# Moving the transfers of the negated maxima from SyncE's queue to ScalarE's in a fused cross-attention and feed-forward kernel

## The reference, cut to what matters

```python
def xattn(q, k, v):            # q = layernorm(x); k = v = ctx; each (16, 128, 256)
    # 8 heads of 16 rows each; positions are the 256 columns
    qh = q.reshape(16 * 8, 16, 256); kh = k.reshape(16 * 8, 16, 256); vh = v.reshape(16 * 8, 16, 256)
    qk = einsum('bdm,bdn->bmn', qh, kh) / sqrt(128 // 8)
    return einsum('bmn,bcn->bcm', softmax(qk, axis=-1), vh).reshape(16, 128, 256)

x = x + xattn(layernorm(x), ctx, ctx)
x = x + routed_expert(layernorm(x), ...)      # top 128 rows for each of 16 experts
x = x + masked_attention(layernorm(x), ctx, mask)
x = x + routed_ffn(layernorm(x), ...)         # top 64 of 128 rows in each batch
```

## Time and profile before

| | |
|---|---|
| median of 3 runs | 457.11 us (456.21 to 458.71) |
| profiled execution | 457.2 us |
| its span | 455.4 us |
| TensorE busy | 350.1 us, 77% |
| VectorE busy | 318.7 us, 70% |
| ScalarE busy | 170.2 us, 37% |
| SyncE's queue (q1) | 32.59 MB, 30.7% of 16 DMA engines |
| ScalarE's queue (q10) | 32 packets, 0.01 MB |
| transfers of the maxima | 30 on SyncE, 2 on ScalarE |
| transfers into the query stack, line 257 | 48 of 128 KB, 7.1 us from issue to landing (median) |

### The profile page before, as it was taken

How to read it: one execution, slowest core, us unless ns; L and a number is a source line. 1 busy time by engine, 2 the same in 40 slices (tenths; PEclk the granted TensorE clock), 3 DMA queues, 4 the chain that set the end, 5 groups by cost and what they waited for, 6 DMA issues and landing times.

```text
span 455.4 us, 7666 instructions
## 1 busy us (share of the span) xinstructions
PE 350.1 (77%) x1872; PEld 204.9 (45%) x1872; DVE 318.7 (70%) x989; ACT 170.2 (37%) x397; POOL 94.4 (21%) x222
## 2 busy tenths in 40 slices
PE   0054997998989999999999994100156999999996
PEld 0021442443534544445444442000134888888884
DVE  6755473887688778886788544788747788878641
ACT  3201553454536444554434441000011355565622
POOL 1101303304214133141110100000013333332300
PEclk9999998999999999999999996555555799999999
DMA  3887591480652815717100009000000000000001
GB/s 95 193 194 126 135 182 21 133 147 18 180 84 69 186 23 143 135 52 153 29 25 1 2 2 356 12 0 1 0 0 2 1 14 11 23 23 23 23 24 48
DMA packets 24363, 32.87 MB, mean 72 GB/s; under 512 B 4066, under 2 KB 22418, under 8 KB 22802
## 3 DMA queue, kind: packets, MB, share of 16 engines
q1 hardware_dynamic: 24306, 32.59, 30.7%
q10 hardware_dynamic: 32, 0.01, 0.0%
HBM read 24.02 MB, written 8.39 MB: 71 GB/s over the span
## 4 chain that ended last, share of the span: by engine, by line
PE 44%; DVE 17%; DMA 16%; issue 8%; SPq 6%; POOL 4%; ACT 3%; DVEq 0%; ACTq 0%; POOLq 0%
PE pv_bank L1041 15%; DMA q_stack<-neg_max 9%; PE t_bank L1247 5%; PE pv_bank L1165 5%; DMA q_parts_dram<-q_parts 4%; PE scoret_bank L1027 4%; PE score_bank L1014 4%; SPq L257 3%; PE t_bank L1069 2%; DMA q_stack<-q_parts_dram 2%; PE score_bank L1228 2%; PE score_bank L1195 1%; DVE junk L668 1%; SPq L238 1%; DVE equal L668 1%
## 5 line engine op out<-in xcount | busy, mean ns | idle before, releaser
L1041 PE MATMUL pv_bank<-probs,values_ones 128*32 128x256 f32 x512 | 135.5, 390 | 0.0
L517 DVE TENSOR_REDUCE row_max<-score_bank 128x2 f32<-128x512 f32 x112 | 75.9, 679 | 54.1 <-PE score_bank L1014 53.0
L858 ACT ACTIVATE probs<-scoret_bank 128x512 f32<-128x512 f32 x128 | 74.4, 593 | 73.9 <-PE scoret_bank L1027 72.9
L1041 PEld LDWEIGHTS pv_bank<-probs,values_ones 128*32 128x32 f32 x512 | 46.0, 110 | 54.4 <-issue 25.7
L1027 PE MATMUL scoret_bank<-q_stack,k_stack 98*128 98x256 bf16 (+1 forms) x256 | 50.3, 279 | 15.8 <-DMA q_stack<-neg_max 13.0
L1014 PE MATMUL score_bank<-k_stack,q_stack 96*128 (+1 forms) x240 | 48.7, 289 | 9.8 <-DMA q_stack<-q_parts_dram 9.8
L357 POOL TENSOR_SCALAR var_eps<-mv 128x1 f32<-128x1 f32 x48 | 9.2, 192 | 191.9 <-DVE mv L553 108.8
L1014 PEld LDWEIGHTS score_bank<-k_stack,q_stack 96*128 (+1 forms) x240 | 17.1, 100 | 48.5 <-issue 24.7
L1027 PEld LDWEIGHTS scoret_bank<-q_stack,k_stack 98*128 98x128 bf16 (+1 forms) x256 | 24.1, 99 | 27.8 <-issue 20.0
L1165 PE MATMUL pv_bank<-q_stack,k_stack 128*128 (+1 forms) x256 | 36.1, 285 | 0.4 <-ACT q_stack L990 0.4
L1165 PEld LDWEIGHTS pv_bank<-q_stack,k_stack 128*128 128x128 f32 x256 | 33.8, 202 | 1.3 <-issue 0.9
(11 more groups left out here) (182 smaller groups left out, 540.6 us busy)
## 6 DMA issues: line engine op xcount, KB each, us to landing
q_stack<-q_parts_dram SPq DMA_DIRECT2D x48, 128.0 KB, 7.1
k_parts_dram<-k_parts SPq DMA_DIRECT2D x24, 128.0 KB
q_parts_dram<-q_parts SPq DMA_DIRECT2D x24, 128.0 KB
k_stack<-k_parts_dram SPq DMA_DIRECT2D x8, 384.0 KB, 4.5
ctx_stage<-in_ctx_dram SPq DMA_DIRECT2D x8, 256.0 KB, 3.3
x_stage<-in_x_dram SPq DMA_DIRECT2D x8, 256.0 KB, 4.1
k_stack<-k_parts_dram SPq DMA_DIRECT2D x8, 256.0 KB, 5.2
xs<-in_x_dram SPq DMA_DIRECT2D x8, 256.0 KB, 2.7
```

The costliest lines, as they stand in the source:

```text
L517: dve.tensor_reduce(row_max[:, i, :, h], score_bank[h % 2][:, :].rearrange("p (m n) -> p m n", m=2), AX.X, ALU.max).then_inc(s["max_done"], 1)
L858: act.activation(probs[:, j % 4, :], scoret_bank[j % 2][:, :], ACT.Exp).then_inc(s["exp_done"], 1)
L1041: ins = pe.matmul(pv_bank[i][pair * Q:(pair + 1) * Q, odd * D:(odd + 1) * D], values_ones[:, i, k, pair, odd, :], probs[:, j % 4, k * D:(k ...
```

## The change

SyncE no longer issues any transfer of the maxima. ScalarE issues all of them, each pair behind a wait for `neg_done`: the odd batch's in step 2, between the exponential and `take_xnt`, and the next unit's even batch's in step 11, behind the exponential. The opening pair stays where it was, written with the new helper. The query stack's six pieces of 16 rows are as before; only the unused variable `n` goes.

```diff
@@ SyncE: load_stacks and the unit @@
-                n = NH * 2 * D
                 sp.dma_start(k_to[0:3 * C], k_rows).then_inc(s["stacks_loaded"], 16)
...
                 for block, part in enumerate((0, 0, 0, 1, 1, 2)):
                     sp.dma_start(q_to[block * C:(block + 1) * C], q_rows[part]).then_inc(s["stacks_loaded"], 16)
-
-            def load_neg_max(u, i):
-                wait_apart(sp, s["neg_done"], 2 * u + i + 1)
-                for part in range(2):
-                    sp.dma_start(q_stack[QROWS + part:QROWS + part + 1, u % SLOTS, :, i, :],
-                                 neg_max[:, i, part, :]).then_inc(neg_loaded[i], 16)
...
             def unit(u, more_stage, more_parts, more_x, reused):
-                load_neg_max(u, 1)
                 if more_x:
...
                     load_stacks(u + 2, reused)
-                if more_x:
-                    load_neg_max(u + 1, 0)
@@ ScalarE @@
+            def load_neg_max(b, u, i):
+                act.wait_ge(s["neg_done"], b + 1)
+                for part in range(2):
+                    act.dma_start(q_stack[QROWS + part:QROWS + part + 1, u % SLOTS, :, i, :],
+                                  neg_max[:, i, part, :]).then_inc(neg_loaded[i], 16)
...
             neg_high(0, 0, 0)
-            act.wait_ge(s["neg_done"], 1)
-            for part in range(2):
-                act.dma_start(q_stack[QROWS + part:QROWS + part + 1, 0, :, 0, :],
-                              neg_max[:, 0, part, :]).then_inc(neg_loaded[0], 16)
+            load_neg_max(0, 0, 0)
...
                     if j == 0:
                         neg_high(2 * u + 1, u, 1)
+                    if j == 2:
+                        load_neg_max(2 * u + 1, u, 1)
                     if j == 2 and not first:
                         take_xnt(2 * u - 2, 0, second)
...
                     if j == 9 and not last:
                         neg_high(2 * u + 2, u + 1, 0)
+                    if j == 11 and not last:
+                        load_neg_max(2 * u + 2, u + 1, 0)
```

## The result

The changed kernel takes 461.40 us (median of 20 runs, 457.69 to 468.43), the kernel before 456.38 (20 runs, 452.57 to 460.07): ratio 1.0103, 95% interval 1.0074 to 1.0132. The forecast was 456.5, with a range up to 461.0. A second series of the same kernel, beside other experiments, gave 463.23 (6 runs) and a ratio of 1.017 (1.0122 to 1.0217).

A forecast was written before the change was run, and what follows sets the result against it. TensorE, busy nearly throughout attention, was taken to wait most for the maxima's transfer. Stalls shortened by 4.0 us less ScalarE's 3.3 us loss gave -0.7 from 457.2, so 456.5 us, range 451.0 to 461.0.

The forecast's parts named there:

- case B: The forecast itself: stacks drain first, ScalarE's cost and the earlier writes about cancel; 456.5 us; chance 0.45.
- What bounds the kernel, and the price of the stalls: Attention stage: TensorE nearly always busy, its largest wait the maxima's transfer; 7.2 us could go, plus 1.6 from low clock.
- Part 1: Even maxima on ScalarE, step 11: issue hidden, stacks still drain first; gain 0.1 us in units 1-4, 0.6 in unit 0.
- Rival A: The second queue overtakes the stacks: gain 7.2 + 1.6, loss 3.3, net -5.5, 451.7 us; chance 0.30.
- Part 2: Odd maxima on ScalarE, step 2: cast of q delayed, TensorE loses 0.4 us in six units, 3.3 in all.
- Part 3: SyncE without its wait issues x and k writes earlier, q writes meet emptier engines: each stall 0.7 us shorter, bound 1.3.
- The sum: Stalls lose 1.1 us in unit 0, 2.9 in units 1 to 4; gain 4.0, loss 3.3: -0.7, 456.5 us.
- Rival C: ScalarE's step 2 issue pair costs 1.96 us or more: 6.9 lost, 3.0 gained with x between; +3.9, 461.1 us; chance 0.20.
- The signs: Maxima waits near 9 us mean case B; issues 650 to 800 ns; exponential wait at step 3 grows 0.5 to 0.9.
- The stacks as next limit: Stacks becoming late for the next unit's scores: some 3 us in hand, about 2 without the stall; within the remaining 0.05.

The follow-up runs named there:

- experiment 10: Changed kernel with x behind the maxima, high part issued before the low-part wait, last three query-stack pieces held until ScalarE issued the even maxima: 448.68 us, ratio 0.9836.
- experiment 2: Kernel before, with only the even batch's maxima issued by ScalarE, in step 11: 454.39 us, ratio 0.9987.
- experiment 7: experiment 2's kernel, with the last two query-stack pieces held on SyncE until ScalarE has issued the maxima: 452.19 us, ratio 0.9909 to the kernel before.
- experiment 1: Kernel before, with only the odd batch's maxima issued by ScalarE in step 2, SyncE keeping its wait for them: 457.89 us, ratio 1.0046.
- experiment 4: Changed kernel with SyncE's wait for the odd maxima put back, so x is behind the even maxima: 456.97 us, ratio 1.0045 to the kernel before.
- experiment 3: Kernel before, with the load of x moved on SyncE directly behind the stacks, ahead of the even batch's maxima: 458.63 us, ratio 1.0060.
- experiment 6: experiment 4's kernel, with ScalarE issuing each pair's high part ahead of the wait for the low part: 451.26 us, ratio 0.9881 to the kernel before.
- experiment 9: Changed kernel, x still ahead, with ScalarE issuing each pair's high part ahead of the low-part wait: 454.34 us, ratio 0.9955 to the kernel before.

## Why the prediction was wrong

The forecast was case B, 456.5 us, with a gain of 4.0 and a loss of 3.3 us. The loss came about as sized, the gain did not come.

- **What bounds the kernel, and the price of the stalls**: right in kind. Without them the kernel is 1.6% faster (experiment 10, 7.5 us; I had 7.2 + 1.6).
- **Part 1, a second queue does not overtake**: right, shown by experiments 2 and 7. That the issue at step 11 costs TensorE nothing: right too, experiment 2 is not slower. Rival A is refuted.
- **Part 2, ScalarE's issues at step 2**: the mechanism is right, and the total is right partly by luck. I had 1.5 us for a pair, and it took 1.50. I had 3.3 us in all, and the first halves of units 1 to 6 lose 3.2. But the single unit loses 0.66 us in units 2 to 4 and not 0.4, since about 0.2 us pass between the wait's end and the first issue and again behind the second; units 1 and 5 lose 0.3 to 0.4, and unit 7, where I had 0.3, nothing (203.3 us from its start to the end in both). The bounds of that sum mix two ways of counting units 6 and 7; by the single terms they are 1.9 and 11.5 instead of 1.6 and 12.4, and nothing rests on it.
- **Part 3, SyncE no longer waits**: this step failed. I credited each stall with 0.7 us from emptier engines and kept x's 256 KB, now next to the maxima, only as a bound. The writes did gain: from the first q write to the first stack issue it takes 5.15 us, mean of units 0 to 4, for 5.66 before, so 0.5 us. But x took it back: the last packet of the maxima starts 1.75 us behind the last of the stacks for 0.92, so 0.8 us more. From the first q write to the landing of the maxima the five units took 17.99 us on average before and 17.90 in the change, where I had 0.7 less. With x behind the maxima again the stalls are shorter (3.24 us in experiment 1 and 2.27 in experiment 4 for 6.42, though the profiled executions lie 2.4 and 1.4 us below their medians), with the same write gain of 0.5 us. Experiment 3 gives x alone 2.7 us, experiment 4 gives 2.6 back when x goes behind the maxima again.
- **The sum**: the cost of ScalarE's issues net of the writes' gain is 2.1 us (experiment 1), that of x is 2.7 (experiment 3), together 4.8; the change lost 4.7 in its first series (1.03%) and 7.8 in its second, and I had -0.7. The sum is a rough one: both experiments have the writes' gain of 0.5 us a unit in them (5.14 and 5.19 us), and the change has it only once. Rival C had the mechanism of x in between and its sign, but tied it to an issue pair of 1.96 us, which did not occur. Its chance of 0.20 was too low, because one half of it needed no condition: that SyncE runs past its old wait and issues x at once follows from the order of the queue.
- **The signs**: the waits for the maxima are 13.3 us and not near 9, which by itself says that the gain is missing; the issues took 658 to 742 ns but for the first, as for B; the wait for the exponential at step 3 grew to 1.17 us and not 0.9.
- **The stacks as next limit**: no run shows TensorE waiting for them inside the units.

What stays open: why experiments 6 and 9 gain more than the first halves explain, why the change lost 1.0% in one series and 1.7% in the other, and the scatter of about 1 us of single landings.

## What to carry to other kernels

Taking a wait out of a queue lets everything behind it go sooner: look at what comes next in that queue, how large it is and which small, urgent transfer it now precedes. An urgent transfer is helped by its place in the order of issue, not by a queue of its own: two pieces of a large load issued behind it instead of ahead gained 0.8 points (experiments 2 and 7), the move to the other queue by itself nothing. On a compute engine an issue costs nothing while the engine would wait anyway, and delays all that follows it when it stands behind a wait that ends late; split off the part that is ready sooner.

## What the runs showed of the hardware

In these runs the transfers of both queues were worked off nearly in the order in which they were issued. A pair of 4 KB transfers on an otherwise empty queue landed 6.8 to 8.8 us behind the last issue of 1.5 MB on the other one (experiment 2 and the change); in experiment 2 none of its packets started sooner than 3.6 us behind its first issue. Holding back the issue of 256 or 384 KB on one queue until the small pair was issued on the other brought the pair's last packet in 1.1 and 1.7 us ahead of the last of the large load, so the order counts across queues. A transfer of 4 KB takes ScalarE about 0.66 us to issue, as it takes SyncE, and its first one took 1.29.
